# 396 instead of 240 maximum units in the first layer, and a 72-step order for TensorE with 81 units

## What is computed

```python
q = (x @ Wq.T).reshape(d, n, h)        # d = 128, n = 3327, h = 8
k = (x @ Wk.T).reshape(d, n, h)
v = (x @ Wv.T).reshape(d, n, h)
a = jnp.einsum('dnh,dmh->dnm', q, k) * scale
a = a + spatial_encoding + edge_encoding      # both are adj
a = jax.nn.softmax(a, axis=2)
out = jnp.einsum('dnm,dmh->dnh', a, v)
return out.reshape(n, h * d) @ Wo.T
```

## Time and profile before

| | us |
|---|---|
| median of 3 runs (lowest, highest) | 14013.82 (14008.34, 14019.46) |
| time of the profiled execution | 14010.76 |
| its span, first to last instruction | 14008.8 |
| TensorE matmul busy | 13478.1 (96%) |
| VectorE busy | 13232.8 (94%) |
| ScalarE busy | 13081.8 (93%) |
| mean granted TensorE clock | 0.991 |

### The profile page before, as it was taken

The page is one execution under the profiler, slowest core; times in us unless marked ns, Lnnn a source line. Parts: engine busy times, 40 slices in busy tenths (PEclk is TensorE's granted clock), DMA queues, the critical chain, the costliest instruction groups (busy, mean ns, idle before and its releaser), DMA issues. The chain is left out here.

```text
span 14008.8 us, 336678 instructions
## 1 busy us (share of the span) xinstructions
PE 13478.1 (96%) x130699; PEld 4160.9 (30%) x130699; DVE 13232.8 (94%) x27589; ACT 13081.8 (93%) x26706; POOL 327.0 (2%) x945
## 2 busy tenths in 40 slices
PE   4789999999999999999999999999999999999998
PEld 3422222222222222222222222222222222222224
DVE  5679999999999999999999999999999999999992
ACT  1259999999999999999999999999999999999997
POOL 1100000000000000000000000000000000000000
PEclk8989999999999999999999999999999999999999
DMA  8975655656565565656566565656656565665653
GB/s 270 253 169 139 147 138 139 148 138 148 138 147 138 141 147 137 149 138 148 137 140 147 138 148 138 148 138 142 145 138 148 138 148 138 142 144 138 147 137 92
DMA packets 2000897, 2067.13 MB, mean 148 GB/s; under 512 B 809017, under 2 KB 1757280, under 8 KB 1992896
## 3 DMA queue, kind: packets, MB, share of 16 engines
q1 hardware_dynamic: 1999006, 2043.37, 62.0%
q10 hardware_dynamic: 288, 2.23, 0.0%
HBM read 1922.23 MB, written 122.68 MB: 146 GB/s over the span
## 5 line engine op out<-in xcount | busy, mean ns | idle before, releaser
L239 DVE CUSTOM_DVE_ANT_0 swept<-X,adj_row 128x832 f32<-128x832 f32 x13312 | 12833.4, 1021 | 228.5 <-PE X L261 156.9
L990 ACT ACTIVATE prob<-S 128x476 f32<-128x476 f32 x23296 | 11597.9, 569 | 169.8 <-PE S L1052 58.9
L1074 PE MATMUL O<-prob,v_pad 128*32 128x238 f32 (+1 forms) x77648 | 6678.7, 416 | 22.0 <-ACT o_sb L1013 19.2
L1052 PE MATMUL S<-q_blk,k_res 52*128 52x476 f16 x23296 | 5963.4, 368 | 19.8 <-ACT S L981 8.0
L261 PE MATMUL X<-mk,mq 40*128 40x416 f16 x26624 | 5752.1, 344 | 185.8 <-DVE m_part L239 116.9
L1052 PEld LDWEIGHTS S<-q_blk,k_res 52*128 52x128 f16 x23296 | 1666.2, 93 | 3494.7 <-ACT prob L990 1470.6
L261 PEld LDWEIGHTS X<-mk,mq 40*128 40x128 f16 x26624 | 1537.6, 93 | 3263.8 <-DVE m_part L239 2778.1
L1074 PEld LDWEIGHTS O<-prob,v_pad 128*32 128x32 f32 x77648 | 1528.5, 108 | 2663.2 <-issue 2404.4
L981 ACT ACTIVATE S<-adj_key 128x476 f32<-128x476 f32 (+1 forms) x2912 | 1701.2, 584 | 30.7
L239 DVE DVE_READ_ACCUMULATOR2_ANT m_part<- 128x1 f32 x13312 | 1105.0, 83 | 0.0
L211 POOL TENSOR_SCALAR m_neg<-m_full 128x16 f32<-128x16 f32 x208 | 52.5, 253 | 12596.5 <-DVE m_full L222 12596.4
(11 more groups left out here) (86 smaller groups left out, 1045.4 us busy)
## 6 DMA issues: line engine op xcount, KB each, us to landing
adj_row<-in_adj SPq DMA_DIRECT2D x1600, 416.0 KB, 3.8
adj_key<-adj_by_key SPq DMA_DIRECT2D x2496, 238.0 KB, 3.9
mk<-k_planes SPq DMA_DIRECT2D x1664, 104.0 KB
adj_key<-adj_by_key SPq DMA_DIRECT2D x416, 236.0 KB, 3.8
mk<-k_planes SPq DMA_DIRECT2D x1664, 52.0 KB
row<-in_adj SPq DMA_DIRECT2D x47, 1663.5 KB, 8.2
adj_by_key<-aT SPq DMA_DIRECT2D x26, 1664.0 KB, 11.8
q_planes<-q_parts SPq DMA_DIRECT2D x26, 1024.0 KB, 15.0
```

The lines of the kernel that those rows point to most:

```text
L239: nc.vector.tensor_tensor_reduce(out=swept[u % 2][:], in0=x_, in1=adj_row[gi % 4][:].rearrange("p (a b) -> p a b", a=2), scale=1.0, scalar ...
L990: nc.scalar.activation(prob[born(j, d // 4) % QR][:, d % 4, 0:w], S[b][:, 0:w], ACT.Exp, scale=2.0).then_inc(s_e[b], 1)
L1052: nc.tensor.matmul(S[b][:, 0:w], k_res[base:base + KR, d // 2, s * P:(s + 1) * P], q_blk[n % 2][base:base + KR, d // 2, 0:w], start=False, ...
L1074: done = nc.tensor.matmul(O[32 * d:32 * d + 32, cols], v_pad[:, s, 4 * q + d, :], prob[born(j, q) % QR][:, d, cols], start=first, stop=Tru ...
```

## The change

Three things. The first layer takes 396 units: 18 per row tile in place of 12, in 22 tiles from the sixth (t = 5) on in place of 20 from the eighth. `LEAD` goes along, so that 24 units are again sent between the first layer and the loop's first step. And `ORDER` has 72 steps with 81 units in place of 36 with 41. It is made of blocks of 12 steps: block A (14 units) stood twice in the old cycle, followed by a third block with 13 units; the new cycle is A, A, B, A, B, B, with a new block B, also of 13 units. All blocks have 24 fills and 12 half value products.

```diff
-    LEAD = 264
-    EU = 240
-    UT = (2, 2, 1, 2, 2, 1, 2)
-    XT = 7
+    LEAD = 420
+    EU = 396
+    UT = (3, 3, 2, 3, 2, 2, 3)
+    XT = 5
...
-             "x01", "yv0xy1", "0v1", "xyx01", "yV0x1", "yv0xy1", "v0x1", "y0xyv1", "0x1", "yv0x1", "yVxy01", "xy0vxy1v")
+             "xy01", "v0x1", "yv0x1", "yv0x1", "yv0x1", "yV0xy1", "xy0v1", "0x1", "yv01", "xy0x1", "yVxy01", "xy0vvxy1",
...
+             "xy01", "v0x1", "yv0x1", "yv0x1", "yv0x1", "yV0xy1", "xy0v1", "0x1", "yv01", "xy0x1", "yVxy01", "xy0vvxy1")
```

## The result

| | us |
|---|---|
| before, median shown ahead | 14013.82 |
| before, beside these runs | 14009.0 to 14013.3 |
| the change, median of 4 runs (lowest, highest) | 14121.88 (14109.33, 14127.91) |
| ratio to the kernel before, 95% interval | 1.0078 (1.0065 to 1.0091) |
| forecast (range) | 14009 (13935 to 14080) |

A forecast was written before the change was run, and what follows sets the result against it. In the loop, block A was taken as bound by VectorE, the old third block by TensorE's order. First layer +149 and loop -151 on 14010.8 gave 14009 us, no change within 0.2% (28 us); range 13935 to 14080.

The forecast's parts named there:

- The first layer, +149: First layer: 22 tiles of 32.65 us take 718 us where tiles 5 to 26 took 569, costing 149 us.
- the per-tile sum: First-layer tile: six more sweeps, seams and projection chain add 6.4 us to 26.25, so 32.65 us per tile.
- 0.35 of seams: First layer, where TensorE holds a third unit for a sweep: more VectorE idle time, 0.35 us per tile.
- 0.4 on the projection chain: First layer, group 5: product and second half of k stand behind a waiting second unit, 0.4 us per tile.
- The loop, -151: Loop: 72 steps take 79.53 us, from A 13.46 and B 13.05, 0.95 less per cycle, gaining 151 us.
- The letter-by-letter walk: Loop blocks: sweep starts followed through B's order give 13.03 us, taken as 13.05; same walk gives A 13.39.
- The start of the loop, zero: Loop start: four more `v_pad` loads, 3.7 us, offset by 3.8 us more sweeps; VectorE's stall stays 12 us.
- the tail: Last some 190 steps, after VectorE's last sweep: paced by ScalarE alone, unchanged because the units end at the same step.
- (1): Rival: B runs at ScalarE's floor of 12.87 us, gain 237, total 13923 us; chance 0.18.
- (2): Rival: first layer hides the six units like the first twelve, cost +56, total 13916 us; chance 0.14.
- (3): Rival, slower: B stays bound by TensorE's order, 13.2 giving 14080 us or 13.32 giving 14138; chance 0.27.
- The signs named ahead: Checks: last tile's L691 at 913, tiles 32.65 us; wrong if tile under 31 or over 34, B outside 13.0 to 13.1.

The follow-up runs named there:

- fillers: Matmuls with unused results added on TensorE in the first layer; 15 per tile where TensorE waited, against the change: 14056.44 us, ratio 1.0033.
- O: The old cycle's third block, 13 units; put in place of each B in the change: 14172.67 us, ratio 1.0116.
- AAB: The kernel before with only its old third block replaced by the new B, 240 units in the first layer: 13968.99 us, ratio 0.997.

## Where the prediction was right and where it was wrong

**The first layer, +149: wrong, +222.** The step that failed is the per-tile sum, 6 x 0.945 of sweeps, 0.35 of seams and 0.4 on the projection chain: it has no term for TensorE's clock. It took every duration on TensorE from rows of before, thus almost all at the upper clock level, and asked nowhere whether TensorE keeps it once it waits again and again for a sweep. The terms that are in it hold to within 0.5 us: with fillers, and the clock at 0.97 to 0.99, a tile takes 32.58 us for my 32.65. That the two agree to 0.1 us is partly luck, since tiles wholly at the upper level average about 32.1. The missing term is the clock's, at least 35.8 - 32.58 = 3.2 us per tile, 70 us in 22, and by the tiles at the upper level some 3.7 and 82. The rows of before had a sign of it: in the tile that I read, the granted clock was 0.93 against 1.00 in the loop.

**The loop, -151: the mechanism right, the size not, -104.** Per 72 steps 0.63 us were gained where I summed 0.95. B came at 13.12 and not at 13.05: 3 x 0.07 = 0.21. The letter-by-letter walk hits every sweep of the block shown within 0.06. What it leaves out are the reductions and transpositions of every 64 units, which would make up such a difference, and I had seen the same 0.07 in A (walk 13.39, trace 13.46) without adding it to B. A came at 13.52 and not at 13.46, 0.17 in all, where I had taken A as a constant: with O in place of B it is back at 13.47 to 13.49. What an A behind a B waits for was not looked into. The last 0.05 went the other way, the old cycle being 80.53 and not 80.48.

**The start of the loop, zero: right** (13.18 us for 12.18), **and so was the tail** (379 instructions in 180 us, last sweep to last exponential 209 us for 212). The DMAs of the units, costed at nothing, didn't show either: the sweeps of the first layer waited 1.0 us in all for bias rows.

**The rivals.** (1), B at ScalarE's floor, is refuted by 13.12. It drew on the rule that each switch of tiling mode drains TensorE (the Trainium skill, TensorEngine Tiling (Array Packing), Key Properties): B has one visit fewer to the value products, and still it takes 13.12 and not TensorE's sum of 12.23; the one long stop in the block shown is VectorE's behind `V`. What such a switch costs by itself, no run here isolates. (2), the six more units hidden at 0.356 us each, fell with 35.8 us per tile. (3), slower, was the right sign for a wrong reason: it wanted B at 13.11 or more with the first layer at +149. B at 13.12 does carry the sum over the bound of 28 us by a little, as (3) has it, but of the 119 us by which the profiled execution (14127.9) misses the forecast, 47 are the loop's, 33 of them B's, and 73 the first layer's. No case had the clock in it. The signs named ahead did their work: the last L694 was to come at 913 and came at 983, a tile took over 34 us, and B was outside 13.0 to 13.1.

## What to carry to other kernels

Work that is moved has a price where it goes and a worth where it leaves, both per unit, and both change with how many there are: here 0.36 us up to twelve units per tile and 1.5 to 1.6 beyond as it came (about 1 at the upper clock level), against 0.4 in the loop, so the half of the change that touched only the order (AAB) was the better kernel. When a stage is filled up until TensorE waits for another engine, don't cost its work by rows at the upper clock level; look at the granted clock of the stretch before, try fillers to size it, and compare tiles that ran at the upper level throughout with the rest. And if a walk through an order misses a known block by something, add that miss to the unknown block too.

## What the hardware showed that was not expected

- In the tile shown, three waits of TensorE for VectorE of 0.6 to 1.1 us, close together, were followed by its lower clock level. 18 of 20 tiles had stretches at that level, 0.84 to 0.86 on average, and with the waits filled it was 0.97 to 0.99. Its busy time hardly tells the two kernels apart, 148 of 200 us in place of 155 to 157.
- Useless matmuls made this kernel faster: 15 more per tile gave 65 us, while eight in a kernel that didn't need them cost 17. Where they stand decides: 16 per tile in four places, ahead of the third units, gave 18 us, and 15 in eight places gave 65.
